# A decoder layer with an S4D convolution on one core: x read back in four wide reads, and TensorE summing the tables of groups 1 and 5

## The reference

```python
K = 2 * real(einsum('hn,hnl->hl', Ct, exp(dtA * l)))      # S4D taps, 256 channels x 1024, from 64 modes each
y = irfft(rfft(x, 2048) * rfft(K, 2048))[:, :1024]        # long convolution along the sequence
x = layernorm(x + layernorm_wb(x + y + x * D))
x = layernorm(x + cross_attention(x, ctx))                # 16 heads of 16, 77 keys
x = layernorm(x + mlp(x) + product_key_experts(x))        # 1024 experts, top 8 of 64 pair scores, 4 heads
```

## Time and profile before

| | |
|---|---|
| median of 3 runs (lowest, highest) | 672.06 us (670.06, 674.78) |
| the profiled execution's own time | 673.4 us |
| its span in the trace | 671.6 us |
| mean granted TensorE clock | 0.941 |
| busy: TensorE / VectorE / ScalarE / GpSimd | 88% / 72% / 60% / 46% |
| DRAM read, written | 21.42 MB, 10.26 MB |

### The profile page before, as it was taken

The page is one execution under the profiler, slowest core; times in us unless marked ns, Lnnn a source line. Parts: engine busy times, 40 slices in busy tenths (PEclk is TensorE's granted clock), DMA queues, the critical chain, the costliest instruction groups (busy, mean ns, idle before and its releaser), DMA issues.

```text
span 671.6 us, 9797 instructions
## 1 busy us (share of the span) xinstructions
PE 587.7 (88%) x3208; PEld 383.5 (57%) x3208; DVE 486.3 (72%) x955; ACT 404.6 (60%) x597; POOL 309.4 (46%) x354
## 2 busy tenths in 40 slices
PE   6708796995787689999999999999999999899896
PEld 2404475764555454455784754777655488453485
DVE  6996867550577858997667788846879795768782
ACT  4853764330353457977746798664878683687760
POOL 3804758665423555422447252353634342743441
PEclk9857999998897669999999999999999999999998
DMA  8996031576070000000000000000000000000000
GB/s 275 297 235 122 1 104 41 162 187 124 0 288 26 1 0 1 1 0 0 1 1 8 17 1 8 1 0 1 17 8 9 0 1 0 17 8 9 0 9 23
DMA packets 19569, 33.75 MB, mean 50 GB/s; under 512 B 7253, under 2 KB 13911, under 8 KB 18199
## 3 DMA queue, kind: packets, MB, share of 16 engines
q1 hardware_dynamic: 15143, 28.93, 15.5%
q10 hardware_dynamic: 4376, 4.20, 2.2%
HBM read 21.42 MB, written 10.26 MB: 47 GB/s over the span
## 4 chain that ended last, share of the span: by engine, by line
PE 66%; DVE 12%; DMA 8%; ACT 7%; issue 3%; POOL 2%; SPq 1%; DVEq 0%; ACTq 0%; POOLq 0%
PE banks L841 20%; PE banks L933 8%; PE banks L938 8%; PE banks L888 4%; PE banks L910 4%; DMA scr_x<-arena 3%; PE banks L864 3%; PE banks L722 3%; PE banks L900 3%; PE banks L711 3%; PE banks L775 2%; ACT arena L953 2%; DVE stats L1483 2%; PE banks L873 2%; PE banks L925 2%
## 5 line engine op out<-in xcount | busy, mean ns | idle before, releaser
L1306 POOL TENSOR_TENSOR arena<-arena 128x1024 f32<-128x1024 f32 x64 | 123.1, 1924 | 159.2 <-ACT arena L1168 158.4
L841 PE MATMUL banks<-arena 128*128 128x512 f32 x384 | 174.4, 596 | 5.3 <-issue 3.7
L841 PEld LDWEIGHTS banks<-arena 128*128 128x128 f32 x384 | 69.8, 190 | 83.0 <-issue 76.8
L1168 ACT ACTIVATE arena<-arena 128x1024 f32<-128x1024 f32 x64 | 73.5, 1149 | 7.6 <-DVE arena L1571 3.0
L1170 ACT ACTIVATE arena<-arena 128x1024 f32<-128x1024 f32 x64 | 73.5, 1149 | 2.1
L1571 DVE SCALAR_TENSOR_TENSOR arena<-arena 128x1024 f32<-128x1024 f32 x48 | 63.9, 1331 | 1.7
L1279 POOL TENSOR_SCALAR arena<-mv 128x1 f32<-128x1 f32 (+1 forms) x40 | 14.5, 361 | 100.1 <-DVE mv L1484 98.7
L933 PE MATMUL banks<-arena 128*128 128x256 f32 x256 | 58.4, 381 | 2.4 <-DVE arena L1593 2.1
L1056 ACT COPY arena<-banks 128x512 f32<-128x512 f32 (+1 forms) x64 | 34.1, 533 | 42.9 <-PE banks L833 30.8
L938 PE MATMUL banks<-arena 128*128 128x256 f32 x256 | 57.9, 379 | 0.0
L1070 ACT ACTIVATE tok<-tok,arena,rstd 128x256 f32<-128x256 f32 x48 | 27.9, 598 | 47.5 <-POOL arena L1284 46.5
(11 more groups left out here) (179 smaller groups left out, 1098.2 us busy)
## 6 DMA issues: line engine op xcount, KB each, us to landing
scr_x<-arena SPq DMA_DIRECT2D x16, 256.0 KB, 9.6
arena<-scr_x SPq DMA_DIRECT2D x4, 1024.0 KB, 11.2
scr_z<-arena ACTq DMA_DIRECT2D x13, 256.0 KB, 4.2
tok<-in_x SPq DMA_DIRECT2D x8, 256.0 KB, 5.8
arena<-scr_z SPq DMA_DIRECT2D x4, 512.0 KB
out<-tok SPq DMA_DIRECT2D x16, 128.0 KB, 1.7
arena<-scr_z SPq DMA_DIRECT2D x2, 640.0 KB
arena<-in_imat SPq DMA_DIRECT2D x1, 1152.0 KB, 6.7
```

Source lines behind the costliest of these rows:

```text
L841: ins = mm(bk[:, cols_of], w[:, k, P * m:P * m + P], src[:, k, cols_of], start=(k == 0), stop=(k == KC - 1))
L1168: fn(ebuf[m % 2], sxb[m % 2], ACT.Prelu, bias=negt[:, n % 2, h:h + 1], alpha=FAR).then_inc(s_ranked, 1)
L1306: tt(sxb[m % 2], sim[:, n % 2, h, 0:XR].unsqueeze(2).broadcast_to((P, XR, NKEYS)), sim[:, n % 2, FH + h, :].unsqueeze(1).broadcast_to((P, ...
```

## The change

Four things change. (1) The reads of `scr_x`: all 16 writes are waited for, then four reads of 128 partitions by 8 KB (four planes each) are issued, and each `x_second` waits only for the reads that hold its planes; SyncE then waits for all four before it goes on. (2) `V_ON_POOL` loses groups 1 and 5, whose taps take twice the matmuls. (3) `Z_DIRECT` is gone: the last three planes go through `scr_z` too, and the second half gets a fourth batch. (4) Many place numbers and offsets move.

```diff
-Z_BATCHES = (((0, 1, 2), (3, 4), (5, 6), (7, 8)), ((0, 1, 2), (3, 4), (5, 6)))
-Z_DIRECT = (FREQ + 7, FREQ + 8)
-V_ON_POOL = tuple(g for g in range(NGRP) if g % HALF_GROUPS)
+Z_BATCHES = ((0, 1, 2), (3, 4), (5, 6), (7, 8))
+V_ON_POOL = (2, 3, 6, 7)
...
-         "taps": (1.261,), "x_second": (-0.5, 0.7), "skip": (1.248, 0.3), "k_first": (5.915, 0.66, 9.6, 0.247),
+         "taps": (0.811,), "x_second": (-0.542, 0.628), "skip": (1.25, 0.378), "k_first": (5.915, 0.402, 9.6, 0.247),
...
-         "diagonal": (-1.42,), "k_second": (8.773, 0.13, 9.955, 0.1), "spectra": (9.027, 0.13, 10.11, 0.1),
+         "diagonal": (-1.42,), "k_second": (8.702, 0.13, 9.955, 0.113), "spectra": (9.027, 0.13, 10.07, 0.1),
...
-LAG = {("dve", "score"): 0.096, ("act", "score"): 0.206, ("act", "best"): 0.157, ("dve", "attend"): 0.085,
-       ("dve", "expert"): 0.129, ("dve", "inner"): 0.078, ("dve", "outer"): 0.141, ("dve", "spread"): 0.104,
+LAG = {("dve", "score"): 0.096, ("act", "score"): 0.232, ("act", "best"): 0.157, ("dve", "attend"): -0.009,
+       ("dve", "expert"): 0.129, ("dve", "inner"): 0.04, ("dve", "outer"): 0.141, ("dve", "spread"): 0.104,
...
-            def x_back(a):
-                sp.wait_ge(s_xaw[a], 16 * 4)
-                sp.dma_start(xS[2 * NS * 2 * a:2 * NS * 2 * (a + 1), 0:NSLOT, :].rearrange("p r n -> p (r n)"),
-                             t["scr_x"][a].rearrange("b c s r n -> (b c s) (r n)")).then_inc(s_xb, 16)
-
             for j, q in enumerate(Q_ORDER):
                 sp.wait_ge(s_xae, 2 * (j + 1))
                 for h in range(2):
                     sp.dma_start(t["scr_x"][q % QUAD, q // QUAD, h].rearrange("s r n -> (s r) n"),
-                                 cA[:, h, q, :]).then_inc(s_xaw[j // 2], 16)
-                if j % 2 and j > 1:
-                    x_back(j // 2 - 1)
-            x_back(QUAD - 1)
+                                 cA[:, h, q, :]).then_inc(s_xaw, 16)
+            sp.wait_ge(s_xaw, 16 * 2 * NQ)
+            for i in range(QUAD):
+                r = slice(QUAD * i, QUAD * i + QUAD)
+                sp.dma_start(xS[:, r, :].rearrange("p r n -> p (r n)"),
+                             t["scr_x"][:, :, :, :, r, :].rearrange("a b c s r n -> (a b c s) (r n)")).then_inc(s_xb[i], 16)
+            for i in range(QUAD):
+                sp.wait_ge(s_xb[i], 16)
...
             def x_second(k1):
                 pe.wait_ge(s_mat, 16)
-                pe.wait_ge(s_xb, 16 * QUAD)
+                for i in range(tiles_of(k1)[-1] // QUAD + 1):
+                    pe.wait_ge(s_xb[i], 16)
...
-                    if n in Z_DIRECT:
-                        for j, r in enumerate(tiles):
-                            act.dma_start(zB[NS * r:NS * r + NS, hf].rearrange("p h q n -> p (h q) n"),
-                                          zring[:, d, j, :]).then_inc(s_zr[hf], 16)
-                    else:
-                        act.dma_start(t["scr_z"][hf, tiles[0]:tiles[0] + planes].rearrange("r p n -> p r n"),
-                                      zring[:, d, 0:planes]).then_inc(s_zw[d], 16)
+                    act.dma_start(t["scr_z"][hf, tiles[0]:tiles[0] + planes].rearrange("r p n -> p r n"),
+                                  zring[:, d, 0:planes]).then_inc(s_zw[d], 16)
```

More of the change, by code:

```diff
@@ L58 @@
 PAIRS = [(0, NC)] + [(2 * m - 1, 2 * m) for m in range(1, FREQ - 1)] + [(NC - 1,)]
[L61 to L68, removed]
+PLACE = {"probs": (0.166, 0.2594, 0.4414), "score": (0.273, 0.6343), "attend": (0.592,), "turno": (0.772,),
+         "project": (1.4,), "project_last": (0.934,), "turn1": (-0.087, 0.0434), "query": (0.245, 0.2687),
+         "query_first": (-0.08, -0.07, 0.245, 0.2684), "score_first": (0.0, 0.043), "turn2": (-0.052, 0.0811),
+         "sim": (0.379,), "sim_first": (0.031,), "best": (0.432,), "best_first": (0.193,),
+         "pair": (0.283, 0.3905, 0.7926, 0.8032), "total": (0.847,), "first": (-0.1,), "sums": (-0.805,),
+         "exps": (-0.131,), "late": (-0.027, 0.0084, 0.7016),
+         "conv": (-2.338, -1.7113, -1.4966, -1.4189, -1.3282, -1.2895, -1.1708, -0.9581),
+         "ln": (-1.672, -1.4033, 0.3164, 1.2251, 1.9414, 2.374, 3.0362, 3.1449),
@@ L69 @@
          "ln_steps": (-0.501, -0.234, 0.162, 0.013, 0.361), "sines": (-2.943, -2.336), "tables": (0.152,),
-         "taps": (1.261,), "x_second": (-0.5, 0.7), "skip": (1.248, 0.3), "k_first": (5.915, 0.66, 9.6, 0.247),
-         "simw": (-2.4,), "x_bias": (12.0, 0.1), "values": (7.2,), "stage": (-2.151,), "keys": (7.496,),
-         "diagonal": (-1.42,), "k_second": (8.773, 0.13, 9.955, 0.1), "spectra": (9.027, 0.13, 10.11, 0.1),
+         "taps": (0.811,), "x_second": (-0.542, 0.628), "skip": (1.25, 0.378), "k_first": (5.915, 0.402, 9.6, 0.247),
@@ L73 @@
+         "simw": (-2.4,), "x_bias": (12.0, 0.1), "values": (7.21,), "stage": (-2.151,), "keys": (7.496,),
+         "diagonal": (-1.42,), "k_second": (8.702, 0.13, 9.955, 0.113), "spectra": (9.027, 0.13, 10.07, 0.1),
          "inverse": (9.103, 0.13, 10.25, 0.11), "products": (0.0, 1.0, 0.0, 0.996, 0.0, 0.802, -0.084, 0.975),
-         "probs_alone": (0.016, 0.0791, 0.4732), "score_alone": (0.367, 0.6875), "attend_alone": (0.566,),
+         "probs_alone": (0.016, 0.0793, 0.4736), "score_alone": (0.367, 0.6877), "attend_alone": (0.566,),
@@ L82 @@
        ("pool", "best"): -0.307, ("dve", "total"): 0.102, ("pool", "pair"): -0.018, ("dve", "turn1"): -0.015,
-       ("act", "first"): 0.149, ("dve", "taps"): 0.053, ("pool", "norm3"): 0.053, ("pool", "first"): 0.189}
+       ("act", "first"): 0.149, ("dve", "taps"): 0.053, ("pool", "norm3"): 0.053, ("pool", "first"): 0.189,
+       ("dve", "dev3"): 0.001}
 SCRATCH = (("scr_x", (QUAD, 2, 2, NS, NSLOT, B * D)), ("scr_z", (2, NSLOT, P, B * HC)),
@@ L441, in build @@
         s_kq, s_zr = ([sem(f"{n}{h}") for h in range(2)] for n in ("taps_moved", "z_loaded"))
-        s_xb = sem("xb_loaded")
+        s_xb = [sem(f"xb{i}_loaded") for i in range(QUAD)]
         s_xa, s_xae, s_ftap = sem("xa_mm"), sem("xa_evac"), sem("ftap_loaded")
-        s_xaw = [sem(f"xa_written{a}") for a in range(QUAD)]
+        s_xaw = sem("xa_written")
         s_imat = sem("imat_loaded")
@@ L549, in taps_bank @@
             return bank[(4 if hf else 6) + g % 2]
-        def z_loads(hf):
-            return len(Z_BATCHES[hf]) + sum(len(tiles_of(n % FREQ)) for n in Z_DIRECT if n // FREQ == hf)
         def z_writes(upto, d):
@@ L643, in _ @@
             for hf in range(2):
-                for batch in Z_BATCHES[hf]:
+                for batch in Z_BATCHES:
                     for n in (FREQ * hf + k for k in batch):
@@ L812, in conv @@
             def conv(q):
-                pe.wait_ge(s_zr[1], 16 * z_loads(1))
+                pe.wait_ge(s_zr[1], 16 * len(Z_BATCHES))
                 if q not in CONV_EARLY:
@@ L824, in _ @@
             pe.wait_ge(s_ze, 2 * FREQ)
-            pe.wait_ge(s_zr[0], 16 * z_loads(0))
+            pe.wait_ge(s_zr[0], 16 * len(Z_BATCHES))
             for q in CONV_EARLY:
@@ L943, in evac_taps @@
             if i == 0:
-                for a in range(QUAD):
-                    act.wait_ge(s_xaw[a], 16 * 4)
+                act.wait_ge(s_xaw, 16 * 2 * NQ)
             act.wait_ge(s_ktm, i + 1)
```

## The result

The changed kernel takes **671.07 us** as a median of 20 runs (665.24 to 673.38), against 672.28 for 20 runs of the kernel before beside them. The ratio is **0.9967, with a 95% interval of 0.9951 to 0.9983**: about 2.2 us faster, small but outside what the measurement leaves open. The time lies in the range and within 1%; the direction was missed. The profiled execution took 670.99 us with a span of 669.2, against 673.4 and 671.6.

The account below looks back on a forecast made before the run. TensorE was taken to bound the main stage, a relay of DMA waits and engines the head. Terms -0.41 + 1.0 - 1.0 + 1.0 - 0.5 made +0.1, so 672.1 us from a median of 672.06; range 665.5 to 678.

Parts of the forecast that it names:

- the last planes: End of the head: three planes go by DRAM, one more read queues behind; +1.0 us, ends -4.4 and +4.5.
- three cases: New read of the last planes costs what the copies did, 0; copies took no share, +4.5; copies stretched the reads, -4.4.
- signs of being wrong: Taps(0) not earlier, t7 still waiting for GpSimd, or the last scr_z read landing past 170 us.
- The reads of x: Head: with x read earlier, taps(0) starts at 55.35 instead of 60.01 us; -4.66 us.
- The rival in which x lands late: Head: wide reads of scr_x land late and delay taps(0); 680.8 us, or 675.8 in mild form; chance 0.15.
- The clock on taps(0): Head: TensorE idles 3.7 us before taps(0), which then runs partly at 1.2 GHz; +1.0 us, ends 0 and +1.9.
- The doubled taps: Head: groups 1 and 5 take twice the matmuls on TensorE; +2.90 and +1.35 us.
- My -0.41: Sum at the first k_second of earlier x reads and the two doubled groups: -4.66 + 2.90 + 1.35 us.
- The rival of the long tail: End of the head: the extra read queues whole behind two others, +4.5 for +1.0; 675.6 us, chance 0.13.
- The second part: Head's second part: k_second(3) moves into the wait before inverse(0), perhaps keeping the clock up; -1.0 us, ends +0.3 and -1.7.
- the main stage: Main stage: turn2 ahead of a spread starts ScalarE's copies some 0.6 us sooner; -0.5 us, ends -1.5 and +1.0.

Follow-up runs that it names:

- Experiment 5: Kernel before with the three direct copies of the last planes left out and nothing in their place (output wrong): 669.63 us, ratio 0.9954.
- Experiment 6: Changed kernel with the direct copies of the last planes and the old batches back: 671.94 us, ratio 1.0010 to the kernel before.
- experiment 3: Kernel before with only the new place numbers and offsets, so the new order of all lists: 671.07 us, ratio 0.9976.
- experiment 1: Kernel before with only the four wide reads of scr_x and the waits that go with them: 670.67 us, ratio 0.9975.
- experiment 4: Kernel before with only groups 1 and 5 taken off GpSimd and accumulated by TensorE: 677.39 us, ratio 1.0065.
- experiment 9: Kernel before with the wide reads of scr_x and 18 overwritten matmuls before taps(0): 669.68 us, ratio 0.9946.
- experiment 2: Kernel before with only the last three planes sent by DRAM instead of direct copies: 669.93 us, ratio 0.9952.
- experiment 7: Changed kernel with GpSimd summing groups 1 and 5 again: 668.80 us, ratio 0.9947 to the kernel before.
- experiment 8: Changed kernel with 18 overwritten matmuls on TensorE before taps(0): 668.91 us, ratio 0.9944 to the kernel before.
- experiment 10: Changed kernel run once more, unaltered, as a control on the chip of the last runs: 671.20 us, ratio 0.9968 to the kernel before.
- experiment 11: Changed kernel with GpSimd summing groups 1 and 5 again and 18 overwritten matmuls before taps(0): 668.08 us, ratio 0.9934 to the kernel before.
- experiment 12: Experiment 11 plus 12 overwritten matmuls behind the early convolutions and 18 before the first turn1: 664.92 us, ratio 0.9872 to the kernel before.

## Why the prediction was right or wrong

**The failed step: the last planes, put at +1.0.** Of the three cases that I set out there, I took "if the new read costs what the copies did, nothing changes", because "the direct copies and the new read [are] the same bytes to the same partitions". They are the same bytes, and don't cost the same. Measured is -3.2 us alone (interval -5.2 to -1.3), and 2.9 in the changed kernel; both lie inside my ends of -4.4 and +4.5, on the side of the case that I named and didn't take: the copies were what stretched the reads. Experiment 5 tells apart which side of the trade it is. With neither copy nor new read it gains 3.1 (1.4 to 4.8), so the old copies cost some 3 and the route by DRAM, as far as these intervals tell, little. Experiment 6 is the rest of the change without this part: +0.7 us (-0.8 to +2.2), where my other four terms make -0.9. So without the last planes no gain would be left to see. That the copies cost these 3 us is shown by leaving them out; that they do it by stretching the reads beside them, and how, is only read from the traces: in experiment 3 it was a copy itself that landed last.

Where the traces show it: from the start of the last plane's copy-out to the last landing it took 12.13 us before and 11.38, 11.80, 13.99, 11.78 and 11.73 in experiments 1, 3, 4, 6 and 9, all with direct copies. By DRAM it took 10.75 after the change and 10.41, 10.06, 9.95, 10.51, 12.74 and 10.41 in experiments 2, 7, 8, 10, 11 and 12. The medians are 11.79 and 10.41, so 1.4 us. The other half of the 3 us I can't place: in experiment 2 the landing is 1.9 us earlier and `turn1` starts 2.9 earlier. The stretch between the two was 12.80 us before and 11.78 there, but 12.86 after the change; it is 11.6 to 13.0 in all fourteen profiles, shortest where the x32 took 7.17 us, at the full clock, and on both routes.

The profile of before had the row that should have tipped it: the last read took 10.86 us for 512 KB, with the copies and one more read beside it, and a wide megabyte had taken 5.2. I used that row as the price of a narrow read. It was the price of a read in company; the new read of 384 KB, behind everything else, took 5.37 us and not 8.1. None of my signs of being wrong came true either: the band that I gave for the last landing, 164 to 168 us, was so wide that 164.21, where the gain shows, still fell in it.

The Trainium skill (DMA: Bandwidth & Descriptors, Anatomy of one DMA) with 2 us and the bytes at 436 GB/s for each transfer had given 2.3 us for the write and 2.9 for the read, and a sum 1.0 lower. The Trainium skill fits that formula to transfers that GpSimd issues; these are issued by ScalarE and SyncE. Measured are 4.92 and 5.37, so its durations are short by about half. Its sum of -0.9 had the right sign, but with 0 for this term and not -3.2. The same page of the Trainium skill (Rules for kernel authors) says that an outermost dimension below 16 confines a DMA to so many engines; the direct copies have 8 outermost. No run here counts the engines of one copy. An estimate by the Trainium skill's formula on that page, at half of its 436 GB/s, is 2.6 us for 128 KB, so half of the engines alone would not make the 11.39 us of experiment 3.

**The reads of x, -4.66: right.** Taps(0) comes 3.75 us sooner. In this profile the table product that releases it ends 0.9 us later than the 55.27 of before, as the whole head stands some 0.9 us later from its first stage on; together that is the 4.66. The gate of the first `x_second` is ScalarE's bank, as put. The rival in which x lands late has fallen: the last read lands 9 us before the bound that I had given it.

**The clock on taps(0), +1.0: right in kind, too small.** It is 2.6 us in the changed kernel (7.62 against 5.00), outside my upper end of 1.9. I had priced it by a short inverse: 1.13 us of work that took 2.08, so about all of it at the lower level. Taps(0) is 5.00 us of work, and so had more to lose; an estimate from 7.62 and 5.00 puts some 5.2 us of it at the lower level, and the windows have 0.50 and then 0.76. The gap was not "as long" either, 4.30 us against 2.54. Experiment 1 shows the same loss (7.48), and in experiments 8 and 9, with the gap filled, the same matmuls take 5.00. VectorE, whose tables of group 2 wait for taps(0), still waits 2.77 us for it, where I had named 0.2.

**The doubled taps, +4.25: right for the old kernel, too much for the new one.** Alone they cost 4.4 us; that my sum met it is partly luck, as the trace has 2.30 and 1.82 us for the two groups and I had 2.90 and 1.35. In the changed kernel, taking them away gained 0.20% of the time (0.10% with fillers, 11 against 8), both within the intervals. By the traces they cost 2.69 there: group 5 falls to 0.39, as it fills two waits of the new order, of 1.09 and 0.91 us, where I had counted one of 1.55.

With these sizes the first `k_second` adds up: -4.66, the 0.9 of the later head, 2.58 for the clock (7.62 against 5.04), 2.30 and 0.39 make +1.51, and it came 1.53 us later. My -0.41 and the clock's +1.0 had made +0.59.

**The rival of the long tail** is out as well: the last landing is at 164.21, where it would have been past 168.

**The second part, -1.0: right in kind, a little small; the main stage, -0.5: not shown.** Together they are -1.6 in experiment 3, with an interval of -3.2 to 0. From the first `k_second` to the `k_first` at 122 us it took 13.87 us before and 12.38 both in experiment 3 and after the change, 1.49 less, which leaves nothing to see for the main stage. In the changed kernel the wait before `inverse(0)` is 1.33 us shorter and the clock after it stays at 1.00. `inverse(1)` no longer takes 2.08 us.

**The sum.** The single parts make -1.7 - 3.2 - 1.6 + 4.4 = **-2.1 us**, the whole -2.2. That agreement is partly luck: without the doubling the parts make -6.5, and experiment 7 measured -3.6. The intervals are too wide to show that gap by itself; the trace shows the part of it that lies in the doubled taps, 4.12 us alone and 2.69 in the new order. By the terms as they stood, -0.41 + 1.0 - 1.0 + 1.0 - 0.5, the last planes alone account for more than the miss (4.2 of 2.3 us), and the clock term (1.6 too low) gives some of it back.

**What stays open:** where the second half of the 3 us of the last planes lies; what in the direct copies is slow; why the doubled taps cost 2.7 us at the first `k_second` in the new order and only 0.7 to 1.3 by the ratios (in experiment 11's profile the last write and read, 6.07 and 6.20 us, took most of the lead back); and where experiment 12 gains after 188 us.

## What to carry to other kernels

Before you price a moved transfer like the one it replaces, ask what ran beside each row that you take its price from: a read that was slow beside copies may owe it to the copies. A gap in front of a compute-bound stretch is paid twice, in waiting and in the clock afterwards, and a lead that opens a gap can give more than half of itself back (2.44 of 4.08 us in experiment 1); idle matmuls in the gap are cheap where their operands and a bank are there anyway. Single parts tested alone need not add up when they share a gap, so undo them in the new kernel too.

## What the runs showed of the hardware

- A copy of 128 KB from 128 partitions of one tile into 8 of another took 11.39 us at the end of the head, and a read of 512 KB beside such copies took 10.86, 10.11, 10.42 and 10.48 us in four kernels (8.51 in experiment 4, where it was issued later behind them), against 4.61 in experiment 5, with neither the copies nor another read beside it.
- The last read of 384 KB by DRAM took 4.67 to 5.37 us in six profiles and 6.20 in a seventh (experiment 11). That is no less than the 4.61 of 512 KB in experiment 5.
- The fp32 `taps` (x64) take 5.00 us at the higher clock and 7.38 to 7.99 us after 3.88 to 4.55 us without a matmul, in five profiles (the change, experiments 1, 6, 7 and 10). After 18 fillers they took 5.00 to 5.03 in four (8, 9, 11, 12).
- 30 fillers in two more places brought the median from 668.08 to 664.92 us (experiments 11 and 12), without moving any other work. The clock loss is not all gone: in the thirteen other profiles the granted clock between 200 and 260 us is 0.63 to 0.91 by stretches of 20 us.
